# Transposing the inputs of two heads together, and a new order of transposes and copies, in a long-filter and feed-forward kernel

## The reference: what is computed

```python
K = 2.0 * einsum('hn,hnl->hl', Ct, exp(P)).real      # a filter of 1024 taps for each of 64 heads
y = irfft(rfft(u, n=2L) * rfft(K, n=2L))[..., :L]    # causal convolution of each row with its head's filter
y = (y + u * D[:, None]) * mask                      # mask: position < length of the batch
...
def qlinear(x, w):                                   # both sides rounded to 8-bit steps, a scale per row
    return einsum('bsh,oh->bso', fake_quant(x, axis=-1), fake_quant(w, axis=1))
h = silu(qlinear(y, w_gate)) * qlinear(y, w_up)      # w_gate, w_up: 2752 x 1024
out = x + qlinear(h, w_down)                         # w_down: 1024 x 2752
```

## Time and profile before

| | us |
|---|---|
| median of 3 runs (1338.51 to 1340.16) | 1339.59 |
| the profiled execution, its own time | 1339.14 |
| its span on the core | 1336.9 |
| PE busy | 1263.6 (95%) |
| DVE busy | 918.1 (69%) |
| ACT busy | 409.0 (31%) |
| POOL busy | 345.0 (26%) |

### The profile page before, as it was taken

How to read it: one execution, slowest core, us unless ns; L and a number is a source line. 1 busy time by engine, 2 the same in 40 slices (tenths; PEclk the granted TensorE clock), 3 DMA queues, 4 the chain that set the end, 5 groups by cost and what they waited for, 6 DMA issues and landing times.

```text
span 1336.9 us, 20250 instructions
## 1 busy us (share of the span) xinstructions
PE 1263.6 (95%) x6837; PEld 686.5 (51%) x6932; DVE 918.1 (69%) x1536; ACT 409.0 (31%) x593; POOL 345.0 (26%) x326
## 2 busy tenths in 40 slices
PE   2499999999996999999999999999999999999997
PEld 0377777776664444444444444444444444444443
DVE  7677877777884865677656777566776567765675
ACT  2244444444451222322222222222222222222322
POOL 3333333324450122221122211222112131122220
PEclk9799999999998999999999999999999999999999
DMA  3279999997974132323323333223332223322323
GB/s 98 75 243 265 273 265 266 271 296 240 264 221 158 32 68 67 71 67 87 74 62 71 71 77 84 61 69 73 78 84 61 69 69 74 86 67 65 71 60 79
DMA packets 137595, 161.52 MB, mean 121 GB/s; under 512 B 101645, under 2 KB 101855, under 8 KB 136287
## 3 DMA queue, kind: packets, MB, share of 16 engines
q1 hardware_dynamic: 137566, 161.16, 44.7%
HBM read 113.28 MB, written 25.49 MB: 104 GB/s over the span
## 4 chain that ended last, share of the span: by engine, by line
PE 67%; issue 0%; DVE 0%; ACT 0%
PE ps_g L1062 23%; PE ps_u L1062 22%; PE ps_o L1088 22%; PE ps_o L1095 1%; PE ps_t L1072 0%; ACT h_t L1197 0%; DVE ps_o L1149 0%; DVE res L1152 0%
## 5 line engine op out<-in xcount | busy, mean ns | idle before, releaser
L1226 POOL TENSOR_TENSOR h_int<-h,rounder 128x512 bf16<-128x512 f32 x186 | 174.4, 952 | 706.2 <-ACT h L1188 703.4
L1062 PE MATMUL ps_g<-wgu,rows 128*128 128x512 bf16 (+1 forms) x1516 | 327.1, 358 | 5.9 <-PEq L413 4.9
L1062 PE MATMUL ps_u<-wgu,rows 128*128 128x512 bf16 (+1 forms) x1493 | 324.4, 356 | 2.3
L1088 PE MATMUL ps_o<-wd,h_t 128*128 128x512 bf16 x1314 | 294.0, 379 | 1.8 <-issue 0.2
L1182 ACT ACTIVATE g_buf<-g_buf 128x512 f32<-128x512 f32 x192 | 112.3, 585 | 583.7 <-DVE g_buf L1120 583.7
L1120 DVE SCALAR_TENSOR_TENSOR g_buf<-ps_g,sx_all,wide 128x512 f32<-128x512 f32 x192 | 132.3, 689 | 229.6 <-PE ps_g L1062 229.6
L853 PE MATMUL ps_y<-u,toep 128*128 128x512 f32 (+7 forms) x1024 | 268.6, 416 | 2.4 <-ACT s_rows L722 1.0
L1062 PEld LDWEIGHTS ps_g<-wgu,rows 128*128 128x128 bf16 x1536 | 145.2, 98 | 163.5 <-issue 13.2
L1062 PEld LDWEIGHTS ps_u<-wgu,rows 128*128 128x128 bf16 x1536 | 147.0, 98 | 151.6 <-issue 1.0
L853 PEld LDWEIGHTS ps_y<-u,toep 128*128 128x128 f32 x1024 | 176.9, 191 | 89.3 <-issue 57.9
L1088 PEld LDWEIGHTS ps_o<-wd,h_t 128*128 128x128 bf16 x1346 | 131.1, 98 | 151.9 <-issue 1.1
(11 more groups left out here) (141 smaller groups left out, 657.6 us busy)
## 6 DMA issues: line engine op xcount, KB each, us to landing
toep<-k_rev SPq DMA_DIRECT2D x64, 512.0 KB, 5.7
res<-in_x SPq DMA_DIRECT2D x64, 256.0 KB, 3.9
out_x<-res SPq DMA_DIRECT2D x64, 256.0 KB, 3.2
wide<-in_L_ffn_w_gate SPq DMA_DIRECT2D x22, 512.0 KB, 6.6
wide<-in_L_ffn_w_up SPq DMA_DIRECT2D x22, 512.0 KB, 8.4
wide<-in_L_ffn_w_down SPq DMA_DIRECT2D x8, 1376.0 KB, 8.5
rows<-in_x SPq DMA_DIRECT2D x32, 256.0 KB, 6.6
x_more<-in_x SPq DMA_DIRECT2D x32, 256.0 KB, 7.0
```

The source lines that it names most:

```text
L1062: last = pe.matmul(bank[:, 0:n], xq[:, par, c, :], wgu[:, NC - 1 - c, first + cols.start:first + cols.stop], start=(c == 0), stop=(c == NC ...
L1088: last = pe.matmul(ps_o[o][:], h_t[0:width, c, :], wd[0:width, c, o * W:(o + 1) * W], start=(c == 0), stop=(c == FC - 1))
L1226: pool.tensor_tensor(h_int[:, piece(j)], h[:, par, piece(j)], rounder[:].to_broadcast([P, n]), ALU.subtract).then_inc(h_int_ready, 1)
```

## The change

Three edits, all in the second part.

1. `turn_x` took the 64 rows of one head at a time: 8 transposes of 64 rows by 128 positions for hh 0 behind the first convolution of a tile, and 8 more for hh 1 behind the second. Now it takes all 128 rows (both heads) and one half k of the positions: 4 transposes of 128 by 128 for k = 0 and 4 for k = 1, both behind the first convolution. `take_u` copies each half and sorts the heads apart; u has two buffers by the tile's parity, and both convolutions wait for both copies.
2. On PE `turn_max` and `spread_inv` stood right behind a convolution, ahead of turn_x and turn_w. Now they stand behind turn_w, last before the next convolution.
3. On ACT both take_u stand together. In the down stage `round_down(i+1)` stood ahead of the copies of pieces 0 and 1 (`place_w`); now it stands behind them.

The core of the diff:

```diff
-            def turn_x(i, par, hh):
-
-                rows = slice(hh * B, (hh + 1) * B)
-                for c in range(NC):
-                    last = pe.transpose(ps_x[hh][:, c * B:(c + 1) * B], x_bufs[par][rows, c * P:(c + 1) * P], ident[rows, rows])
+            def turn_x(par, k):
+                for c in range(NC // 2):
+                    first = (k * NC // 2 + c) * P
+                    last = pe.transpose(ps_x[k][:, c * P:(c + 1) * P], x_bufs[par][:, first:first + P], ident[:])
                 last.then_inc(x_turned, 1)
...
-                pe.wait_ge(u_done, 2 * i + hh + 1)
+                pe.wait_ge(u_done, 2 * i + 2)
...
                 for hh in range(2):
                     convolve(i, par, hh)
-                    if not last_one:
+                    if not last_one and hh == 0:
                         await_x(i + 1, 1 - par)
+                        for k in range(2):
+                            turn_x(1 - par, k)
+                    if gate_stage(i) or down_stage(i):
+                        turn_w(i, par, hh if gate_stage(i) else 2 * hh)
+                        if hh == 0 and not gate_stage(i):
+                            turn_w(i, par, 1)
                     if not isinstance(i, int) or i >= 1:
                         if hh == 0:
                             turn_max(i - 1)
                         else:
                             spread_inv(i - 1)
-                    if not last_one:
-                        turn_x(i + 1, 1 - par, hh)
-                    if gate_stage(i) or down_stage(i):
-                        turn_w(i, par, hh if gate_stage(i) else 2 * hh)
-                        if hh == 0 and not gate_stage(i):
-                            turn_w(i, par, 1)
```

```diff
-            def take_u(i, hh):
-                act.wait_ge(x_turned, 2 * i + hh + 1)
-                if not isinstance(i, int) or i >= 1:
-                    act.wait_ge(conv_done, 2 * i + hh - 1)
-                act.activation(u[:, hh, :], ps_x[hh][:], ACT.Copy).then_inc(u_done, 1)
+            def take_u(i, par, k):
+                half = slice(k * NC // 2, (k + 1) * NC // 2)
+                act.wait_ge(x_turned, 2 * i + k + 1)
+                if not isinstance(i, int) or i >= 2:
+                    act.wait_ge(conv_done, 2 * i - 2)
+                act.activation(u[:, par, :, half, :], ps_x[k][:].rearrange("p (c h b) -> p h c b", h=2, b=B),
+                               ACT.Copy).then_inc(u_done, 1)
...
                 if has(i, TILES - 1):
-                    take_u(i + 1, 0)
-                if not gate_stage(i) and has(i, WEIGHT_ITERS - 1):
-                    round_down(i + 1, 1 - par)
+                    take_u(i + 1, 1 - par, 0)
+                    take_u(i + 1, 1 - par, 1)
...
                 elif down_stage(i):
                     place_w(i, par, 0)
                     place_w(i, par, 1)
+                if not gate_stage(i) and has(i, WEIGHT_ITERS - 1):
+                    round_down(i + 1, 1 - par)
```

More of the change, by code:

```diff
@@ L428, in convolve_and_pack @@
         s_rows = sb("s_rows", [GU_UNITS + DOWN_TILES, P])
-        u = sb("u", [P, 2, NC * B])
+        u = sb("u", [P, 2, 2, NC, B])
         y = sb("y", [P, 2, NC, 2, B])
@@ L687, in place_w @@
                 act.activation(wd[:, NC * k:NC * k + whole, cols], bank[:, 0:whole, :], ACT.Copy).then_inc(w_placed, 1)
-            for hh in range(2):
-                take_u(0, hh)
+            for k in range(2):
+                take_u(0, 0, k)
             round_gu(0, 0, 0)
@@ L710, in body @@
                     place_w(i, par, 1)
+                if not gate_stage(i) and has(i, WEIGHT_ITERS - 1):
+                    round_down(i + 1, 1 - par)
                 if gate_stage(i):
                     place_w(i, par, 0)
-                if has(i, TILES - 1):
-                    take_u(i + 1, 1)
                 if gate_stage(i):
@@ L849, in convolve @@
                 out = ps_y[hh][:].rearrange("p c b -> p (c b)")
+                ahead = u[:, par, hh].rearrange("p c b -> p (c b)")
                 for dist in range(NC):
@@ L852, in convolve @@
                     n = (NC - dist) * B
-                    last = pe.matmul(out[:, dist * B:NC * B], toep[:, slot, block_cols], u[:, hh, 0:n],
+                    last = pe.matmul(out[:, dist * B:NC * B], toep[:, slot, block_cols], ahead[:, 0:n],
                                      start=(dist == 0), stop=(dist == NC - 1), skip_group_check=True)
@@ L887, in _ @@
             await_x(0, 0)
-            for hh in range(2):
-                turn_x(0, 0, hh)
+            for k in range(2):
+                turn_x(0, k)
             def body(i, par):
```

## The result

| | before | changed |
|---|---|---|
| median of 4 runs, us | 1339.73 (1338.51 to 1340.16) | 1320.35 (1316.72 to 1321.60) |
| ratio | | 0.9852, 95% interval 0.9831 to 0.9873 |
| the profiled execution | 1339.14 | 1316.72 |
| its span | 1336.9 | 1313.9 |

The change makes the kernel 19.4 us faster; I had forecast 15.7. The profiled execution is the fastest of four, 22.4 us under the one before. I account for these 22.4 first and come back to the spread of 5 us, which the kernel before does not have.

A forecast was written before the change was run, and what follows sets the result against it. PE's queue bounds the gate stage, a closed loop through DVE's maximum and rounding the down stage. Gains of 8.8 (gate), 6.4 (down), 0.6 and 0.7, less 0.8, make 15.7 us: median 1324 us, forecast alone 1319 to 1329.

The forecast's parts named there:

- a closed loop in the down stage: Down stage: maximum, turn_max, turn_x, turn_w, convolution, mask_y, scaling, rounding wait on each other in turn; 12.01 us a tile.
- The pause that I allowed for: PE, gate stage: possible pause where fp32 transposes stand directly ahead of bf16 ones, between zero and some 0.1 us, twice a tile.
- The reserve of 0.06 for the pause: Gate stage, turn_x: a saving of 0.55 us a tile was taken, where at most 0.61 was possible.
- the 0.15 for meetings with POOL: Gate stage: PE loses about 0.6 us in every fourth tile when DVE's rounding stands behind POOL, 0.15 a tile on average.
- The drift that I described: Gate stage: after a held-up rounding, the next tiles round between POOL's pieces and DVE catches up 0.3 us a tile.
- The meeting: Gate stage: DVE's rounding (7.85 us) meets the start of POOL's second piece (7.8); if POOL is first, rounding stands 1.9 us.
- the port as a rival: Gate stage: rounding meets POOL's second piece in each tile, 11.9 us a tile, 1357 us in all; chance 0.06.
- a sign of being wrong: Listed among the signs against the forecast: PE waits for DMA of x ahead of turn_x; no size given.
- the DMA rival: Both stages: denser mix makes packets slower, gate tiles near 10.6 us, down tiles near 11.5, 1332 us; chance 0.18.
- The floor of 10.8 us a tile: Down stage: DMA engines have 0.90 x 12.01 = 10.8 us of work a tile, taken as the lowest possible.
- So the move costs nothing: ACT, down stage: round_down behind two copies delays POOL's start 0 to 0.5 us, hidden by DVE's work; taken as nothing.
- The ends: First convolution waits for both copies of x, +0.8 us; ahead of tile 23, -0.6, and ahead of tile 31, -0.7.

The follow-up runs named there:

- the second profile: The changed kernel run once more, unaltered, on the same chip beside the follow-up kernels: 1319.1 us, ratio 0.9843 to the kernel before.
- both moves on the queue: Changed kernel with loads of x issued ahead of the weights and the second head's Toeplitz load behind both, on the sync engine's queue: 1313.9 us, ratio 0.9807.

## Why the prediction was right, and where not

**The direction and the range were right**, and what bounds each stage was read rightly: PE's queue in the gate stage, a closed loop in the down stage. The forecast of 15.7 us is under the 19.4 of the medians and the 22.4 of the profile. Of the latter the gate stage gave 14.0, where I had 8.8.

**turn_x.** Predicted 0.89 us for eight wide transposes, measured 0.88. The pause that I allowed for between fp32 transposes and bf16 ones isn't there (150.40 is 8 x 0.11 behind 149.52). The 275 ns a transpose of the Trainium skill (TensorE: Matmul & The Clock Gate, Part 4: PE-mode transpose), which spoke for +22 us, are near what one record lasts here (0.27), and not the distance of two.

**The gate stage's gain is mis-sized**: 0.40 us a tile predicted, 0.72 measured in a tile without trouble and 0.67 on average. 0.62 is turn_x; 0.10 I had not seen: a convolution takes 3.94 to 3.95 us instead of 4.00 when an fp32 operation and not a bf16 one stands ahead of it. With edit 2 undone, where turn_w stands ahead again, it is back at 4.00. The reserve of 0.06 for the pause was not used. Of the 0.15 for meetings with POOL the first profile used 0.04, and the second 0.17, waits for x included. The drift that I described, 0.3 us a tile until a border is missed, is there in the second profile with 0.27. What I had not seen is that it can stop: in the first profile the rounding sits at the border of the two pieces for twelve tiles on end, where each time the rounding takes 0.69 us and POOL's second piece 2.4, and POOL then keeps PE's pace of 10.05. A missed border there made its tile 0.4 us longer.

**The meeting was seen, its condition not.** I gave the port as a rival 0.06 and 11.9 us a tile, for the changed kernel. There it does not come; with the paired transposes alone it does, at 11.79. My 11.9 was worked out with a late turn_max, so that it is so near is luck. The missing step is which edit prevents it. I wrote of edit 2 that it costs nothing in the gate stage, and looked there for what it makes late, not for what it lets be late: with turn_max early a missed border is paid by PE and repeats itself, with turn_max 1.33 us later it is for the most part covered. That is worth 32.5 us (1351.6 against 1319.1 beside it), more than the whole gain.

**The down stage.** 11.1 predicted, 10.97 measured, by other terms: the rounding is at 0.69 to 0.72 us in every tile, better than assumed, and PE waits for x for 3.2 us in all, which I had named as a sign of being wrong. It is small, and it is not what the DMA rival said, slower packets: over the down stage the DMA engines moved 277 GB/s where it was 249, and putting the load of x first took the wait away. The floor of 10.8 us a tile, "which is the lowest a tile can be", is wrong: the changed kernel has tiles of 10.39 us, and with both moves on the queue the mean is 10.42, at a share of 0.90 and 298 GB/s. I had taken 0.90 from one stretch, where the seven tiles before have 0.83, and had taken the busy share for a fixed amount of work. So 11.1, set above that floor, was near the 10.97 in part by luck.

**"So the move costs nothing"**, of round_down, is the step that is wrong. Undone, it costs 7.6 us against the changed kernel beside it (1327.0 and 1319.1). I had priced what the move does to round_down and not what the old place does to the copies: they free the bank in which the third piece is transposed.

**The ends.** The first convolution started 1.2 us later (62.63 for 61.40) and ended 0.6 later, as more of it runs at the full granted clock, which returns at about 66 us in both profiles: 0.8 predicted. From spread_inv to the convolution of tile 23 it was 2.30 us and is 1.42; ahead of tile 31 the stretch from the end of the convolution before was 2.60 and is 1.54. That is 0.9 and 1.1 us, where I had 0.6 and 0.7.

## What to carry over

Before shortening the engine that bounds a loop, write down what the other engines deliver into it and how late each may be: a faster queue can close a loop that had been open, and a perfect saving of 0.6 us a tile became a loss of 1.0. Place the instruction that waits for another engine's result last in its group, behind all work that needs nothing. And price a reordering from both sides, also by what the old order held up.

## What the runs showed of the hardware that I had not expected

- VectorE's fp32 to bf16 tensor_scalar of 128x1024 takes 0.69 us, and up to 2.41 when it arrives during a GpSimd tensor_tensor: it ends 0.55 us behind the end of that instruction. It is let in between two GpSimd instructions that would follow directly, and the second then takes 2.25 to 2.44 instead of 1.89 us. The fp32 tensor_tensor with one operand in PSUM (1.21 us) did not change under the same overlap.
- Eight fp32 transposes of 128x128 follow each other at 0.11 us though each record lasts 0.27.
- A group of 64-row transposes between 128-row operations costs some tenths of a us beyond its blocks: 1.50 us for two groups of eight (one head each), 1.07 for one of sixteen. In the group of sixteen the second head's eight add 0.31 us.
- A convolution (sixteen fp32 matmul records) takes 4.00 us behind a bf16 transpose and 3.94 to 3.95 behind an fp32 operation.
- The DMA engines' busy share is not a fixed amount of work: seven down tiles of 12.01 us had 0.83 at 249 GB/s, seven of 10.42 had 0.90 at 298.
- One pause of PE of 1.78 us in the down stage was followed by 3.4 us at half clock, and one of 2.12 us (in the kernel with sixteen narrow transposes) by a granted clock of 0.51 over 7 us. Pauses of 1.70 and 1.77 us in the same stage of other tiles were not, nor were those of 1.45 us once a tile in the gate stage. What decides between them is open.
